# First chunk of a Mamba scan block: gate half of the input projection moved ahead, next chunk's norm moved ahead, first spreads on three queues

## The chip, the cores and the metric

The program runs on one core of one Trainium2 chip. The metric is the device time of the whole program in microseconds (us). The engines are TensorE (PE; its weight loads are shown as PEld), VectorE (DVE), ScalarE (ACT), GpSimd (POOL) and SyncE (SP), which only issues transfers here. A row's `granted clock` is the share of TensorE's full speed of 2.4 GHz: 1.00 is 2.4 GHz, 0.50 is 1.2 GHz.

## The reference

A decoder layer on x of 1 x 2048 x 256: x is added to a Mamba block, then to a cross attention over 1601 context rows, then to a mixture of experts. The change is in the Mamba block alone:

```python
x = x + _L0_attn_ref(_layernorm(x), W_in, conv_w, conv_b, W_x, W_dt, b_dt, A_log, D, W_out)

xz = x @ W_in                                   # 256 -> 1024
x_proj, z = jnp.split(xz, 2, axis=-1)           # 512 channels each
xc = causal depthwise convolution of x_proj, 4 taps
x_conv = silu(xc + conv_b)
dt_in, B_ssm = jnp.split(x_conv @ W_x, 2, -1)   # 16 each
dt = softplus(dt_in @ W_dt + b_dt)
A = -exp(A_log)                                 # 512 x 16
h = h * exp(dt * A) + dt * B * x_conv           # for each step, channel and state
y = sum over states of h + x_conv * D
return (y * silu(z)) @ W_out
```

## The kernel before

`scan_block` computes the Mamba block and takes the first half of the program; `attend_and_route` does the rest after it. The 2048 rows are taken in four chunks of 512 (`NQ = 4`, `CH = 512`, index q). The 512 channels are four blocks of 128 (`KM = 4`, index m). A chunk has 64 scans (`TILES = 64`), each of 128 (channel, state) pairs by 512 steps, numbered t = 0 to 255 over the four chunks. A tile t holds 32 channels by 4 states: n = t // 16 counts blocks of 128 channels, s = t // 4 groups of four scans that share four states, j = t % 4 the 32 channels.

For each scan t:
- ACT makes exp(dt * A) in a PSUM bank (L464), five banks ahead at most (`NDA = 5`: it waits for scan t - 5).
- POOL makes dt * B * x for two scans in one instruction (L296), from `rep` and `b_rep`.
- DVE scans (L567).
- After each four scans PE sums the states into a bank `psY` (`add_states`, L769 and L772). After sixteen of them DVE multiplies `psY` by silu(z) (`gate`, L524), at t = 18, 34, 50, 66 and so on, two scans after the sixteen end.

`rep` holds dt and u = dt * x_conv of each channel copied to four rows of partitions. It is filled by transfers from `dt_u` to `rep` (`spread`, L206): four of 128 KB for each j, sixteen for each n. All are issued by SP, except those of n = 0, j = 3, which POOL issues.

The work that prepares chunk q (`front`) lies among the scans of chunk q - 1 in an order written out by hand. Every step has a slot number k, and `front_time(q, k)` turns it into the scan t before or after which it stands on its engine: for q >= 2 it is 64 (q - 1) - 20 + k, for q = 1 it is 4 + k * 3 // 5. The steps are: transposes of the normed rows (`PE_XNT`), their copy to SBUF (`ACT_XT`, L350), the x half of the projection (`PE_X`, L608, copied by L320), the convolution as four matmuls with diagonal weights for each m (`PE_C`, L623, copied by L361), one silu over the four blocks with a table load before and after it (`ACT_SILU`, L366 and L367), the z half (`PE_Z`, L608, copied by L326), its silu with two table loads (`ACT_ZS`, L336 and L337), the small product (`PE_XS`), the spread of B (`PE_BR`, L332) and the softplus of dt (`PE_V`, `ACT_V`, `DVE_DT`). All of it uses two PSUM banks, `psF`. Each engine runs its own instructions in order, so a step that has to wait holds up all that stands behind it on its engine, the exps of ACT among them.

For the first chunk nothing can be hidden. In order: SP loads x (rows 0 to 511), the x half of `W_in`, the small tensors, the z half of `W_in`, the other 1536 rows, `W_out`. DVE takes the moments (L495, L498), POOL the power (L259, L261), DVE norms (L505) and copies `pick` out of `ident` (L532), while POOL builds `conv_d` (L271). PE transposes and makes the x half. ACT evacuates and makes the first tap (L438), DVE the other three (L538), twelve instructions. ACT's silu (L442) is followed by the small product (L643), its copy (L444), the step sizes (L653), the softplus on DVE and ACT (L552, L554, L448, L450, L516, L518) and the spread. After those PE makes the z half of chunk 0 (L608 again), ACT copies it between the first exps (`evac_z`, at t = 2, 3, 5, 6) and makes its silu at t = 12:

```python
ACT_Z0, ACT_ZS0 = (2, 3, 5, 6), 12
```

DVE takes the moments of chunk 1 after the convolution and norms its rows just before scan 0, where POOL has already made the power.

## Time and profile before

| | us |
|---|---|
| median of 3 runs | 770.64 (767.15 to 771.59) |
| the profiled execution, its time | 765.8 |
| its span in the trace | 764.0 |
| first scan starts | 49.25 |
| last scan ends | 409.3 |
| `attend_and_route` starts | 413.9 |

All rows are of one profiled execution. Its time is 1.8 us more than its span, and it is 4.8 us under the median of the three runs. A line of the timeline gives start, length, engine, line of code, operation and shapes, the count of instructions that are merged, and in brackets how long the engine was idle before it and what ended that.

### The profile page before, as it was taken

The numbers are of one execution on the slowest core, as the hardware profiler recorded it, in microseconds if no ns is written. First come the engines' busy times: TensorE is split into PE (matmuls) and PEld (weight loads), VectorE is DVE, ScalarE is ACT, GpSimd is POOL, SyncE is SP. The second block draws the span as 40 slices with busy tenths as digits, with TensorE's granted clock in tenths as the row PEclk, the third lists the DMA queues.
The fourth block names the chain that finished last, engine by engine and source line by source line (L and its number), as shares of the span: only waits on it lengthen the run. The fifth ranks groups of instructions, "written<-read, shape, count | busy, mean of one in ns | idle before, by whom it ended". The sixth has DMA issues, their size and how long they took to land. (4 is left out here: it accounts for less than half of the span.)

```text
span 764.0 us, 10447 instructions
## 1 busy us (share of the span) xinstructions
PE 636.9 (83%) x3130; PEld 399.2 (52%) x3130; DVE 591.7 (77%) x1040; ACT 445.8 (58%) x795; POOL 475.6 (62%) x391
## 2 busy tenths in 40 slices
PE   4589875997689975577889799999999989899990
PEld 2133212352133510043536799999998964688860
DVE  5787798889998999999887776767888777444327
ACT  2668799676987888848772445444445331444420
POOL 4069599978997999999873433232445347166550
PEclk9799985999869996579999999999999999999996
DMA  7092244325344352943322845442524033445318
GB/s 202 9 220 57 54 111 110 79 46 131 76 110 111 82 133 62 241 107 88 88 87 92 230 148 183 130 163 80 187 87 152 14 98 127 131 152 165 105 35 299
DMA packets 61604, 91.33 MB, mean 120 GB/s; under 512 B 13573, under 2 KB 46536, under 8 KB 61550
## 3 DMA queue, kind: packets, MB, share of 16 engines
q1 hardware_dynamic: 51278, 74.62, 37.5%
q0 software_dynamic: 3936, 8.72, 3.2%
q10 hardware_dynamic: 6336, 7.34, 2.7%
q8 instruction: 26, 0.43, 0.2%
q14 instruction: 28, 0.23, 0.1%
HBM read 36.54 MB, written 22.62 MB: 77 GB/s over the span
## 5 line engine op out<-in xcount | busy, mean ns | idle before, releaser
L296 POOL TENSOR_TENSOR b_in<-rep,b_rep 128x1024 f32<-128x1024 f32 x128 | 299.0, 2357 | 41.4 <-DVE h L567 34.4
L567 DVE TENSOR_TENSOR_SCAN h<-ps,hlast,b_in 128x512 f32<-128x512 f32 x256 | 306.4, 1264 | 16.9 <-ACT ps L464 10.0
L464 ACT ACTIVATE ps<-rep,neg_a 128x512 f32<-128x512 f32 x256 | 171.0, 684 | 42.7 <-DVE h L567 38.8
L772 PE MATMUL ps<-h,pick 128*32 128x512 f32 x512 | 80.5, 705 | 43.4 <-DVE h L567 43.1
L608 PE MATMUL ps<-xnT,w_in 128*128 128x512 f32 x128 | 68.4, 681 | 10.1 <-ACT xnT L350 4.1
L1071 POOL DMA_INDIRECT rows_by_token<-yt,yrow x46 | 44.7, 972 | 43.7 <-ACT yt L1183 19.0
L1212 DVE TENSOR_TENSOR p_lo<-ps,p_hi 128x512 fp32r<-128x512 f32 x64 | 35.1, 592 | 36.0 <-ACT p_hi L1082 36.0
L1480 PE MATMUL ps<-v_hi,p_hi 128*128 128x256 f32 x208 | 60.0, 288 | 1.2 <-DVE x_res L1335 1.2
L772 PEld LDWEIGHTS ps<-h,pick 128*32 128x32 f32 x512 | 10.7, 115 | 94.7 <-DVE h L567 85.0
L1480 PE MATMUL ps<-v_lo,p_hi 128*128 128x256 f32 x208 | 58.5, 281 | 0.0
L1480 PE MATMUL ps<-v_hi,p_lo 128*128 128x256 f32 x208 | 58.3, 280 | 0.0
L608 PEld LDWEIGHTS ps<-xnT,w_in 128*128 128x128 f32 x128 | 26.4, 217 | 51.7 <-issue 40.0
L1082 ACT ACTIVATE p_hi<-ps 128x512 fp32r<-128x512 f32 x64 | 30.0, 516 | 37.4 <-PE ps L1497 37.2
L1678 PE MATMUL ps<-w_exp,xT 128*128 x184 | 44.1, 383 | 0.0
L623 PE MATMUL ps<-xp,conv_d 128*128 128x512 f32 x96 | 43.8, 601 | 0.0
L1480 PE MATMUL ps<-c_hi,q_hi 128*128 128x512 f32 x96 | 41.0, 427 | 0.8 <-PEq L122 0.8
L1443 DVE TENSOR_TENSOR ht<-sgt,ps 128x256 f32<-128x256 f32 x23 | 9.7, 422 | 40.6 <-ACT sgt L1175 40.6
L1052 POOL TENSOR_TENSOR attn_rstd<-attn_mv,eps 128x1 f32<-128x1 f32 x14 | 4.1, 291 | 58.3 <-DVE attn_mv L1205 58.3
L1480 PEld LDWEIGHTS ps<-v_hi,p_hi 128*128 128x128 f32 x208 | 39.2, 188 | 1.4 <-DVE x_res L1335 1.4
L1044 POOL TENSOR_TENSOR rstd3s<-mv3s,eps 128x1 f32<-128x1 f32 x16 | 3.6, 223 | 57.5 <-DVE mv3s L1341 57.5
L1028 POOL DMA_INDIRECT rows_by_block<-xn,pos x32 | 32.4, 1013 | 11.1 <-issue 10.5
L1480 PEld LDWEIGHTS ps<-v_lo,p_hi 128*128 128x128 f32 x208 | 39.3, 189 | 0.0
(265 smaller groups left out, 1356.9 us busy)
## 6 DMA issues: line engine op xcount, KB each, us to landing
rep<-dt_u SPq DMA_DIRECT2D x252, 128.0 KB, 2.4
mask_sb<-in_mask_BxSxS_ik_dram SPq DMA_DIRECT2D x16, 800.5 KB, 4.6
xt<-rows_by_block SPq DMA_DIRECT2D x23, 258.0 KB, 2.8
rows_by_block<-pad SPq DMA_DIRECT2D x4, 1032.0 KB, 9.2
rows_by_token<-pad ACTq DMA_DIRECT2D x4, 1024.0 KB, 6.1
yb<-rows_by_token SPq DMA_DIRECT2D x4, 512.0 KB, 4.8
yb<-rows_by_token ACTq DMA_DIRECT2D x4, 512.0 KB, 5.6
w_exp<-L_ffn_expert_gate_w_dram SPq DMA_DIRECT2D x15, 128.0 KB
```

The source lines that it names most:

```text
L296: pool.tensor_tensor(b_in[:, (t - 1) % NB:(t - 1) % NB + 2, :], u_rep[:, n % 2, j - 1:j + 1, :], b_rep[q % 2][:, g, :].unsqueeze(1).to_bro ...
L464: act.activation(psA[:, t % NDA, :], dt_rep[:, n % 2, j, :], ACT.Exp, scale=neg_a[:, k:k + 1]).then_inc(exp_ready, 1)
L567: dve.tensor_tensor_scan(h[:, QC * (s % NH) + j, :], psA[:, t % NDA, :], b_in[:, t % NB, :], hlast[:, k:k + 1], ALU.mult, ALU.add).then_in ...
L608: last = pe.matmul(psF[:, m % 2, :], w_in[:, n, part * DI + m * P:part * DI + (m + 1) * P], xnT[:, n, :], start=(n == 0), stop=(n == KE - 1))
L623: last = pe.matmul(psF[:, m % 2, :], conv_d[:, m, n, :], xp[:, m, n:n + CH], start=(n == 0), stop=(n == NTAP - 1))
L772: last = pe.matmul(psY[32 * j:32 * j + 32, :], pick[:, :], h[:, QC * (s % NH) + j, :], start=False, stop=(g == NG - 1))
L1028: pool.indirect_dma_start(xs_dram[:, :], bass.IndirectOffsetOnAxis(ap=pos[:, t, k:k + 1], axis=0), xn3[:, t, :], None, bounds_check=NTILE ...
L1071: pool.indirect_dma_start(y_dram[:, :], bass.IndirectOffsetOnAxis(ap=yrow[:, 2 * s + a:2 * s + a + 1], axis=0), yt[:, s % YT, a, :], None, ...
L1082: act.activation(p_hi[:, a:b, :], psP[g % 2][:, 0:(b - a) * P], ACT.Copy).then_inc(pthi_ready, 1)
L1212: dve.tensor_tensor(p_lo[:, a:b, :], psP[g % 2][:, 0:(b - a) * P], p_hi[:, a:b, :].bitcast(F32), ALU.subtract).then_inc(ptlo_ready, 1)
L1480: mm = pe.matmul(out, stat[a], mov[b], start=first and n == 0, stop=last and n == 2)
L1678: last = pe.matmul(psG[i % 2][:, a * 2 * FI:(a + 1) * 2 * FI], xT[:, i % 2, cols], w_all[:, ds(e, 1), wcols].rearrange("p a n -> p (a n)") ...
```

## The change

1. The z half of chunk 0 is made right after the x half, straight into four of the five PSUM banks of the exps (the fourth block after the small product). ACT makes its silu from PSUM, block by block, among the silus of the convolution. The copies at t = 2, 3, 5, 6 and the silu with two table loads at t = 12 go.
2. The four step sizes of chunk 0 go to four different banks, one after another, and the four spreads of B follow.
3. DVE takes the moments of chunk 1, `neg_a` and the norm of chunk 1 before the convolution of chunk 0. POOL makes the power of chunk 1 before `conv_d`. The rows of chunk 1 are loaded by a transfer of their own, third in SP's order.
4. The first spreads: of j = 0 two transfers are issued by SP and two by ACT; j = 1 is issued by POOL, j = 2 and 3 by SP. POOL makes the first two scans' input one at a time.
5. Every step of `front(1)` stands three scans earlier: 1 + k * 3 // 5.

```diff
-ACT_Z0, ACT_ZS0 = (2, 3, 5, 6), 12
+POOL_J = 1
 def front_time(q, k):
-    return 4 + k * 3 // 5 if q == 1 else TILES * (q - 1) - SHIFT + k
+    return 1 + k * 3 // 5 if q == 1 else TILES * (q - 1) - SHIFT + k
+        psV = [psF[:, 1, :], psF[:, 0, :], psY, psA[:, KM, :]]
         # spread and SP
-        def spread(eng, n, j):
-            for r in range(QC):
+        def spread(eng, n, j, rows=range(QC)):
+            for r in rows:
             sp_.dma_start(w_in[:, :, 0:DI], ...).then_inc(s_win[0], 16)
+            sp_.dma_start(x_res[:, CHT:2 * CHT, :], xv[:, CHT:2 * CHT, :]).then_inc(x_next, 16)
...
-                for j in range(QC if n else QC - 1):
-                    spread(sp_, n, j)
+                for j in range(QC):
+                    if n == 0 and j == 0:
+                        spread(sp_, n, j, range(0, 2))
+                    elif n or j != POOL_J:
+                        spread(sp_, n, j)
         # gpsimd
             inverse_deviation(0)
-            pool.wait_ge(xn_ready, 1)
+            inverse_deviation(1)
             pool.wait_ge(s_conv, 16 * 2)
...
-            inverse_deviation(1)
             pool.wait_ge(u_ready, 1)
-            spread(pool, 0, QC - 1)
+            spread(pool, 0, POOL_J)
...
-                if j % 2:
+                if t < 2:
+                    pool.tensor_tensor(b_in[:, t, :], u_rep[:, 0, t, :], b_rep[0][:, 0, :], ALU.mult).then_inc(b_ready, 1)
+                elif j % 2:
         # scalar
-            for m in range(KM):
+            def silu_x0(m):
                 act.wait_ge(conv_done, m + 1)
                 act.activation(xc[0][:, m, :], xc[0][:, m, :], ACT.Silu).then_inc(xc_ready, 1)
+            def silu_z0(m):
+                act.wait_ge(z_ps, m + 1)
+                act.activation(zs[0][:, m, :], psA[:, m, :], ACT.Silu).then_inc(z_evac, 1)
+            silu_x0(0)
+            silu_x0(1)
+            silu_z0(0)
+            silu_x0(2)
+            silu_z0(1)
+            silu_x0(3)
+            silu_z0(2)
             act.wait_ge(xs_ps, 1)
             act.activation(xs[:, :], psF[:, 0, :], ACT.Copy).then_inc(xs_ready, 1)
+            silu_z0(3)
             act.preload_act_table_set("natural_log_exp_and_others")
...
+                if m == 1:
+                    act.wait_ge(u_ready, 1)
+                    spread(act, 0, 0, range(2, QC))
...
-                if t in ACT_Z0:
-                    evac_z(0, ACT_Z0.index(t))
-                if t == ACT_ZS0:
-                    silu_z(0)
         # vector: moments(1), neg_a and normalize(1) move from behind the convolution to ahead of it
-                dve.tensor_scalar(dt[:, m, :], psF[:, (m + 1) % 2, :], b_dt[:, m:m + 1], None, ALU.add).then_inc(v_evac, 1)
+                dve.tensor_scalar(dt[:, m, :], psV[m], b_dt[:, m:m + 1], None, ALU.add).then_inc(v_evac, 1)
         # tensor
+                    if q == 1:
+                        pe.wait_ge(br_ready, NG)
                     normal(q)
...
+            pe.wait_ge(s_win[1], 16)
+            for m in range(KM - 1):
+                w_in_product(psA[:, m, :], m, 1).then_inc(z_ps, 1)
             pe.wait_ge(s_small, 16 * 7)
             pe.wait_ge(x_evac, KM)
             small_product(0)
+            w_in_product(psA[:, KM - 1, :], KM - 1, 1).then_inc(z_ps, 1)
+            for m in range(KM):
+                step_size(0, m)
             pe.wait_ge(pick_ready, 2)
-            for m in range(KM):
-                ...
-                step_size(0, m)
-                if m % 2:
-                    pe.wait_ge(v_evac, m)
-                    spread_b(0, m - 1)
-                    pe.wait_ge(v_evac, m + 1)
-                    spread_b(0, m)
-            pe.wait_ge(s_win[1], 16)
-            for m in range(KM):
-                ...
-                w_in_product(m, 1).then_inc(z_ps, 1)
+            for g in range(NG):
+                if g < 2:
+                    pe.wait_ge(v_evac, g + 1)
+                else:
+                    pe.wait_ge(br_ready, g - 1)
+                spread_b(0, g)
+            pe.wait_ge(v_evac, KM)
```

## Rows read from the trace of the kernel before

**Rows 1.** What DVE waited for between the first and last scan, by releaser
```profile
DVE zs L524 <- PE ps L772: 13.9, 6, 4.8
```
**Rows 2.** Timeline of the first chunk's preparation, all engines
```profile
8.88 5.00 DVE L532 COPY pick<-ident 32x32 f32<-32x32 f32 x4
9.04 3.61 POOL L271 TENSOR_TENSOR conv_d<-ident,conv_w 128x2048 f32<-128x2048 f32 x1 [1.50 <-DVE xn L505]
...
12.25 10.16 PE L608 MATMUL ps<-xnT,w_in 128*128 128x512 f32 x16 [1.20 <-ACT xnT L430]
...
25.21 1.67 ACT L442 ACTIVATE xc<-xc 128x512 f32<-128x512 f32 x3
27.33 0.63 ACT L442 ACTIVATE xc<-xc 128x512 f32<-128x512 f32 x1 [0.45 <-DVE xc L538]
28.11 1.94 PE L643 MATMUL ps<-xc,w_x 128*32 128x512 f32 x8 [5.69 <-ACT xc L442]
...
30.84 3.75 PE L653 MATMUL ps<-xs,w_dt 128*128 128x512 f32 x4 [0.80 <-ACT xs L444]
...
32.92 0.75 DVE L552 TENSOR_SCALAR dt_u<-ps,b_dt 128x512 f32<-128x512 f32 x1 [3.12 <-PE ps L653]
...
36.74 0.69 DVE L518 TENSOR_TENSOR dt_u<-dt_u,xc 128x512 f32<-128x512 f32 x1
```
**Rows 3.** Same timeline from 44 us: spreads land, first scan
```profile
46.88 4.66 POOL L296 TENSOR_TENSOR b_in<-rep,b_rep 128x1024 f32<-128x1024 f32 x2 [6.87 <-DMA rep<-dt_u]
...
48.98 0.69 ACT L464 ACTIVATE ps<-rep,neg_a 128x512 f32<-128x512 f32 x1 [1.55 <-DMA rep<-dt_u]
```
**Rows 4.** DVE alone: the scans and their gaps
```profile
49.25 15.39 DVE L567 TENSOR_TENSOR_SCAN h<-ps,hlast,b_in 128x512 f32<-128x512 f32 x13 [3.18 <-POOL b_in L296]
68.30 4.82 DVE L567 TENSOR_TENSOR_SCAN h<-ps,hlast,b_in 128x512 f32<-128x512 f32 x4 [3.66 <-ACT ps L464]
...
78.82 0.69 DVE L524 TENSOR_TENSOR zs<-ps,zs 128x512 f32<-128x512 f32 x1 [1.90 <-PE ps L772]
...
89.05 3.63 DVE L567 TENSOR_TENSOR_SCAN h<-ps,hlast,b_in 128x512 f32<-128x512 f32 x3 [3.65 <-ACT hlast L468]
...
155.16 0.69 DVE L524 TENSOR_TENSOR zs<-ps,zs 128x512 f32<-128x512 f32 x1 [4.81 <-PE ps L772]
```
**Rows 5.** PE alone, chunk 0's scans
```profile
54.73 1.06 PE L772 MATMUL ps<-h,pick 128*32 128x512 f32 x8
...
57.93 3.70 PE L608 MATMUL ps<-xnT,w_in 128*128 128x512 f32 x8 [1.11 <-ACT xnT L350]
...
74.16 3.60 PE L623 MATMUL ps<-xp,conv_d 128*128 128x512 f32 x8
77.69 1.06 PE L772 MATMUL ps<-h,pick 128*32 128x512 f32 x8
...
96.50 1.04 PE L643 MATMUL ps<-xc,w_x 128*32 128x512 f32 x8
```
**Rows 6.** Windows: length, busy time by engine, granted clock, DMA share, GB/s
```profile
25.00:26.00 1.00, 0.00 (x0) 0.00 (x0) 0.96 (x3) 0.99 (x3) 0.00 (x0) 0.62 0.00 0
...
28.10:34.70 6.60, 5.79 (x13) 1.98 (x14) 3.14 (x13) 2.15 (x3) 1.29 (x2) 0.50 0.00 1
```
**Rows 7.** Transfers between 43 and 52 us, all queues
```profile
DMA packets 774, 2.09 MB, mean 233 GB/s; under 512 B 263, under 2 KB 263, under 8 KB 774
```
**Rows 8.** Loads up to 50 us: KB each, median us to landing
```profile
w_in<-in_L_attn_W_in_dram SPq DMA_DIRECT2D x2, 512.0 KB, 4.6
```
**Rows 9.** ACT alone: exps, last conv copy, first exp after silu, chunk 2's rows
```profile
68.70 1.90 ACT L464 ACTIVATE ps<-rep,neg_a 128x512 f32<-128x512 f32 x3
...
82.42 0.69 ACT L361 ACTIVATE xc<-ps,conv_b 128x512 f32<-128x512 f32 x1 [2.75 <-PE ps L623]
...
88.23 0.69 ACT L464 ACTIVATE ps<-rep,neg_a 128x512 f32<-128x512 f32 x1
...
128.98 1.00 ACT L350 ACTIVATE xnT<-ps 128x1024 f32<-128x1024 f32 x1
```

More of the change, by code:

```diff
@@ L198, in rep_sem @@
         def rep_sem(n, j):
-            return rep_pool if n == 0 and j == QC - 1 else rep_in[n % 2][j]
+            return rep_pool if n == 0 and j == POOL_J else rep_in[n % 2][j]
         def rep_count(n, j):
-            return (n // 2 + (0 if j == QC - 1 and n % 2 == 0 and n else 1)) * QC * 16
-        def spread(eng, n, j):
-            for r in range(QC):
+            return (n // 2 + (0 if j == POOL_J and n % 2 == 0 and n else 1)) * QC * 16
+        def spread(eng, n, j, rows=range(QC)):
+            for r in rows:
                 eng.dma_start(rep[32 * r:32 * r + 32, n % 2, j, :, :],
@@ L227, in _ @@
             sp_.dma_start(w_in[:, :, DI:], w["W_in"][:, DI:].rearrange("(k p) n -> p k n", p=P)).then_inc(s_win[1], 16)
[L228 to L229 removed]
+            sp_.dma_start(x_res[:, 2 * CHT:, :], xv[:, 2 * CHT:, :]).then_inc(s_rest, 16)
+            sp_.dma_start(w_out[:, :, :], w["W_out"].rearrange("(m p) n -> p m n", p=P)).then_inc(s_rest, 16)
             for n in range(KM * NQ):
@@ L453, in _ @@
                     evac_b(0, m)
+            act.wait_ge(z_evac, KM)
             act.wait_ge(ident_ok, 2)
@@ L491, in moments @@
             def moments(q):
-                dve.wait_ge(x_in if q == 0 else x_rest, 16)
+                dve.wait_ge(*((x_in, 16), (x_next, 16), (s_rest, 32))[min(q, 2)])
                 dve.wait_ge(xn_ready, q)
@@ L522, in gate @@
                 dve.wait_ge(summed, NG * (n + 1))
-                dve.wait_ge(zs_ready, q + 1)
+                if q:
+                    dve.wait_ge(zs_ready, q)
+                else:
+                    dve.wait_ge(z_evac, KM)
                 dve.tensor_tensor(zs[q % 2][:, m, :], psY, zs[q % 2][:, m, :], ALU.mult).then_inc(gated, 1)
@@ L533, in _ @@
             last.then_inc(pick_ready, 1)
+            moments(1)
+            dve.wait_ge(a_exp, 1)
+            for r in range(QC):
+                rows = slice(32 * r, 32 * r + 32)
+                dst = neg_a[rows, :].rearrange("p (b g j) -> p b g j", b=KM, g=NG)
+                src = a_log[rows, :, :].rearrange("p (b j) (g n) -> p n b g j", b=KM, n=QC)[:, r]
+                last = dve.tensor_scalar(dst, src, -1.0, None, ALU.mult)
+            last.then_inc(consts_ready, 1)
+            normalize(1)
             for m in range(KM):
@@ L541, in _ @@
                 last.then_inc(conv_done, 1)
-            moments(1)
-            dve.wait_ge(a_exp, 1)
-            for r in range(QC):
-                rows = slice(32 * r, 32 * r + 32)
-                dst = neg_a[rows, :].rearrange("p (b g j) -> p b g j", b=KM, g=NG)
-                src = a_log[rows, :, :].rearrange("p (b j) (g n) -> p n b g j", b=KM, n=QC)[:, r]
-                last = dve.tensor_scalar(dst, src, -1.0, None, ALU.mult)
-            last.then_inc(consts_ready, 1)
             for m in range(KM):
                 dve.wait_ge(v_ps, m + 1)
-                dve.tensor_scalar(dt[:, m, :], psF[:, (m + 1) % 2, :], b_dt[:, m:m + 1], None, ALU.add).then_inc(v_evac, 1)
+                dve.tensor_scalar(dt[:, m, :], psV[m], b_dt[:, m:m + 1], None, ALU.add).then_inc(v_evac, 1)
                 dve.wait_ge(v_evac, m + 1)
@@ L557, in _ @@
                     step_and_input(m)
-            normalize(1)
             for t in range(TILES * NQ):
@@ L604, in normal, with w_in_product @@
                 last.then_inc(xnT_ps, 1)
-            def w_in_product(m, part):
+            def w_in_product(out, m, part):
                 for n in range(KE):
-                    last = pe.matmul(psF[:, m % 2, :], w_in[:, n, part * DI + m * P:part * DI + (m + 1) * P], xnT[:, n, :],
+                    last = pe.matmul(out, w_in[:, n, part * DI + m * P:part * DI + (m + 1) * P], xnT[:, n, :],
                                      start=(n == 0), stop=(n == KE - 1))
@@ L617, in x_part @@
                     pe.wait_ge(x_evac, m - 1)
-                w_in_product(m, 0).then_inc(x_ps, 1)
+                w_in_product(psF[:, m % 2, :], m, 0).then_inc(x_ps, 1)
             def convolve(q, m):
@@ L627, in project @@
                 pe.wait_ge(gated, KM * (q + 1))
-                pe.wait_ge(s_wout, 16)
+                pe.wait_ge(s_rest, 32)
                 for m in range(KM):
@@ L652, in step_size @@
                     pe.wait_ge(br_ready, NG * q + m + 3)
-                pe.matmul(psF[:, (m + 1) % 2, :], w_dt[:, m * P:(m + 1) * P], xs[:, :], start=True, stop=True).then_inc(v_ps, 1)
+                pe.matmul(psF[:, (m + 1) % 2, :] if q else psV[m], w_dt[:, m * P:(m + 1) * P], xs[:, :], start=True, stop=True).then_inc(v_ps, 1)
             def spread_b(q, g):
@@ L692, in front @@
                         pe.wait_ge(c_evac, 3 + m)
-                    w_in_product(m, 1).then_inc(z_ps, 1)
+                    w_in_product(psF[:, m % 2, :], m, 1).then_inc(z_ps, 1)
                 if k == PE_XS:
```

14 lines of the change are left out of this document (2 added, 12 removed).

## The prediction

> **What bounds the kernel now.** I first read the timeline for where the scan block starts its scans and ends: scan 0 starts at 49.25 us, scan 255 ends at 409.3. Before that the first chunk is a chain through all engines, with nothing else to do. In between DVE is nearly always scanning. Thirteen scans take 15.39 us, 1.18 us each [rows 4]; POOL, at 4.66 us for four scans' input, runs at the same 1.17 [rows 3]. So I asked next what DVE waits for. The largest sum is the gate, 13.9 us in six waits, for PE's sums of the states [rows 1]. The change can win in two places: the chain up to scan 0, and the gap of 3.66 us ahead of scan 13, where ACT is away for the silu of z with two table loads [rows 4]. Behind these stand three waits that decide what of it arrives. Gate 0 waits 1.90 us for PE at 78.82; scan 24 waits 3.65 us, because ACT is in the silu of the convolution; gate 3 waits 4.81 us for PE at 155.16 [rows 4]. A gain of DVE that ends in one of them is lost. What reaches the end of the block is what PE gains at gate 3, and nothing after that depends on absolute time.
>
> **The change, step 1: up to the first spread.** ACT is first in line. It makes three silus at 0.56 us each (1.67 / 3), is idle 0.45 us until the convolution ends, and makes the last one at 27.33 [rows 2]. Two silus of z now stand ahead of that one: 2 x 0.56 - 0.45 = 0.67 us later. The small product follows. PE had been idle 5.69 us before it [rows 2], its granted clock had fallen to 0.62 in the window at 25 us and stood at 0.50 until 34.7 [rows 6]. So its eight passes took 1.94 us, where eight at full clock take 1.04 [rows 5]. With three z blocks of 1.77 us each (half of a pair's 3.54, below) PE is busy until about 27.6 and idle only about 1.2 us. I take full clock: -0.90. The step sizes used to start 0.79 us after the product (30.84 - 30.05, the copy by ACT); now the fourth z block lies between, 1.77 us: +0.98. The first step size reaches DVE 2.08 us after its start at half clock [rows 2]; it has two passes, each of which loses about 0.43 us when the clock is full: -0.87. The second is then in its bank when DVE wants it; DVE waited 0.23 for it, -0.25. Sum: 0.67 - 0.90 + 0.98 - 0.87 - 0.25 = -0.4 us. The spread, issued at 37.46 when u of block 0 is ready (36.74 + 0.69) [rows 2], is issued at 37.1. Hidden: table load and z silu of block 3 lie under the step size and DVE's first two instructions. With the clock at half the three PE terms would be +0.90 (the product), +1.77 (the z block) and +0.87 (the step size): 3.5 us more.
>
> Moved ahead of the convolution: moments, `neg_a` and norm of chunk 1, 1.8 + 0.9 + 1.4 us on DVE between the picks and the first tap at 17.6. Room is there if nothing blocks. POOL's `conv_d` now runs from about 12.8 to 16.4 instead of 9.0 to 12.7. It took 3.61 us, and the four small copies of `pick` beside it took 5.00 us instead of under a microsecond [rows 2]. These are free now; `neg_a` and the norm lie beside `conv_d` instead. Whether they are held up like a copy no row shows: between 0 and, if the first tap waits for all of POOL's three instructions and then the norm, 1.3 us on the convolution's end, of which ACT's own 0.67 hides half: 0 to 0.65. I take 0, since the norm's 128 x 256 ran at 0.35 us apiece like an instruction at single rate. The Trainium skill (SBUF — State Buffer, on the port pair that DVE and GpSimd share) says that an exclusive lock holds off a DVE instruction in a two-port mode, or with two SBUF inputs, while GpSimd works. The copies agree with it (3.6 us held up); if it also held the norm and first tap the sum would be 0.65 us worse. The extra transfer third in SP's queue puts all behind it back by one issue, 0.5 us; the z half of `W_in`, issued at 9.8 and 4.6 us on its way [rows 8], lands near 15 and isn't wanted before the x half ends at 22.4 [rows 2]; `conv_w`, near 7, isn't wanted before 12.8.
>
> **Step 2: the spreads.** Sixteen transfers of 128 KB make 2.1 MB. From the first issue at 37.46 to the last exp that waited for them (48.98) [rows 3] are 11.5 us, with all queues together at 233 GB/s [rows 7]: 9.0 us plus 2 until the first byte. More queues change the order, not the rate. So j = 0 and 1 come earlier, scans 0 and 1 start at about 45 and 46, but j = 3 lands 11.0 to 11.5 us after the first issue, at 48.3, whoever issues it. POOL then needs 2.33 us for scans 2 and 3: scan 2 at 50.6 instead of 51.6. From there POOL feeds DVE at DVE's own pace, so only 1.0 us is left of 4. The rule of the Trainium skill (DMA: Bandwidth & Descriptors, Issuing engines are not separate DMA queues) is the same: it saves issue time alone. By it, too, the sum is that of the rows. ACT's two issues (about 1.3 us) hold up its copies of B; nobody waits for these before 43.
>
> **Step 3: PE through chunk 0, the step that decides.** Scan 3 ends at 53.0, and PE sums group 0 at once (1.0 us; 54.73 before [rows 5]), as the z blocks no longer stand ahead of it. Then the front of chunk 1. From the first x block at 57.93 to the sum of group 3 at 77.69 PE had no idle time shown: four x blocks, three convolution blocks and two sums in 19.76 us [rows 5]. With the front three scans earlier the fourth convolution block stands before the sum of group 3 (slot 14 instead of 17, the sum at 16), at 3.53 us (77.69 - 74.16). So 54.0 + 19.8 + 3.5 = 77.3 at full clock. The clock isn't full: PE's last work before is the transposes at about 44 to 46, then it waits some 7 us for scan 3. Before the z blocks filled that place. After an idle time of 5.69 us the clock stood at 0.50 for 6.6 us, 28.1 to 34.7, until it was busy again [rows 6]. Half of such a stretch is lost: 3.3 us at most, 0 if the clock doesn't fall. I take 2.5, as PE is now densely busy. The fourth convolution ends at 79.8 (82.2 before), the sum of group 3 at 80.8, and gate 0 is at 80.9 instead of 78.82. DVE has finished scan 18 about 9 us earlier or stands behind ACT, which waits in order for the convolution's blocks. The 3.66 us and the 1.0 us end here.
>
> **Step 4: ACT to the rows of chunk 2.** The copy of the last convolution block goes from 82.42 to 80.0; from it to the first exp after the silu are 5.8 us [rows 9], so 85.8 instead of 88.23. But that exp is number 21, not 24, three more at 0.63 (1.90 / 3 [rows 9]): exp 24 at 87.7, 0.5 us early. From here to 128.98 ACT was nearly never idle: it sets the pace. Its work there is the same, but three scans earlier the copies meet PE waiting for scans: I count 1.3 us for the fourth z block and 1.4 to 1.8 for B and the first dt, against some 2 us of such waits before. Estimate 1.0 more, 0 to 2. Chunk 2's rows are copied at 129.5 instead of 128.98 [rows 9].
>
> **Step 5.** PE works from there to gate 3 without a free stretch, and DVE has 4.81 us to spare [rows 4]. So gate 3, and the end, come **0.5 us later**. The profiled execution's own time is 765.8, so 766.3; on the median, 770.64 + 0.5 = 771.1.
>
> **The rivals.**
> - *Everything arrives.* PE's clock stays up and ACT and PE catch up by themselves, so DVE keeps 1.0 us of the start and the 3.66 us of the gap: -4.7, 765.9. For it: the z work really leaves ACT (four copies, a silu, two table loads). Against it: the order at gate 0, and the 4.81 at gate 3, where DVE has slack already.
> - *Part arrives.* The clock doesn't fall ahead of the first sum, or rises at once: 2.5 less, -2.0, 768.6.
> - *Slower: PE cold at the small product.* If 1.2 us of idle time and ACT's later silu are enough for the clock to be at 0.50 at 28.8, step 1 is 3.5 us longer, and all behind it moves with it: 0.5 + 3.5 = +4.0, 774.7. It decides from a granted clock below about 0.6 there. Against it: the clock was still full 2.9 us after PE's last matmul (idle from 22.4 [rows 2], 0.62 in the window from 25 on [rows 6]).
> - *The change doesn't fill the wait.* If the z half of `W_in` landed after 22.4 it would; it lands 7 us before. Under 0.02.
>
> **How the numbers follow.** My forecast, -1.2 to +2.0 (bounds of the clock, the port and ACT's waits), 0.50. Part arrives, down to -3.8: 0.17. Everything: 0.13. Slower by 2.0 to 3.8 for mixed bounds: 0.08; cold PE: 0.12. 0.5% of the time, 3.85 us, is about what a measurement can tell from no change: faster 0.13, same 0.75, slower 0.12. The range leaves out the case where everything arrives and goes to the cold case: 766.8 to 774.8.
>
> **What would show it.** Right: the spread issued near 37; scan 0 near 45, scan 2 near 50.6; a granted clock of 1.00 at the small product and 0.5 at 53; a wait of DVE before 80 of some 9 us in all, gate 0 at 81; the first exp after the silu at 85.8; chunk 2's rows at 129.5. Wrong: gate 0 before 78; ACT not back to back between 90 and 125; gate 3's wait gone, because then DVE's gains count as well.

## The result and the profile after

| | before | after |
|---|---|---|
| median of 18 runs, us | 769.82 (767.15 to 773.34) | 772.36 (769.45 to 774.67) |
| profiled execution, span, us | 764.0 | 769.9 |

The changed kernel takes 2.5 us more. The ratio is 1.0032 with a 95% interval of 1.0018 to 1.0046, so 1.4 to 3.5 us more: a small loss, under 0.5% of the time, but clear of noise. 0.5 us more had been forecast. All ratios here are of the fast executions alone, which leaves out one single execution, of the kernel best below, that took 3450 us.

The two profiled executions are 5.9 us apart, more than the medians, and 4.3 of that lie behind the scan block, where no line differs. The profiled execution of before (765.8 us, span 764.0) is quicker than all of its 18 runs in the table, so the profiles are compared here only inside the scan block. *Gate n* is DVE's n-th product of the summed states with silu(z), from 0 to 15; a chunk has four.

First DVE alone, the scans (L590) and the gate (L547). It answers to [rows 4].

```profile
44.89 1.27 DVE L590 TENSOR_TENSOR_SCAN h<-ps,hlast,b_in 128x512 f32<-128x512 f32 x1
46.37 1.28 DVE L590 TENSOR_TENSOR_SCAN h<-ps,hlast,b_in 128x512 f32<-128x512 f32 x1 [0.21 <-POOL b_in L298]
50.87 7.16 DVE L590 TENSOR_TENSOR_SCAN h<-ps,hlast,b_in 128x512 f32<-128x512 f32 x6 [3.21 <-POOL b_in L302]
...
71.83 1.28 DVE L590 TENSOR_TENSOR_SCAN h<-ps,hlast,b_in 128x512 f32<-128x512 f32 x1 [2.62 <-ACT ps L488]
...
81.36 0.69 DVE L547 TENSOR_TENSOR zs<-ps,zs 128x512 f32<-128x512 f32 x1 [1.81 <-PE ps L797]
81.97 2.45 DVE L590 TENSOR_TENSOR_SCAN h<-ps,hlast,b_in 128x512 f32<-128x512 f32 x2
87.06 7.16 DVE L590 TENSOR_TENSOR_SCAN h<-ps,hlast,b_in 128x512 f32<-128x512 f32 x6 [2.64 <-ACT ps L488]
...
155.50 0.69 DVE L547 TENSOR_TENSOR zs<-ps,zs 128x512 f32<-128x512 f32 x1 [3.54 <-PE ps L797]
```

Scan 0 starts 4.4 us earlier than before, scan 2 about 0.7, and the gap of 3.66 us ahead of scan 13 is gone. Six smaller waits for ACT stand between scan 2 and gate 0 instead, 8.0 us together, and gate 0 is 2.5 us later. At gate 3 the kernels are 0.3 us apart (155.50 against 155.16). The cause of the late gate stands in PE's rows [rows 5]:

```profile
44.58 1.02 PE L794 MATMUL ps<-xc,skip_d 128*128 128x512 f32 x2
53.38 1.93 PE L797 MATMUL ps<-h,pick 128*32 128x512 f32 x8 [7.78 <-DVE h L590]
55.24 5.50 PE L631 MATMUL ps<-xnT,w_in 128*128 128x512 f32 x8
...
73.16 7.14 PE L646 MATMUL ps<-xp,conv_d 128*128 128x512 f32 x16
80.23 1.06 PE L797 MATMUL ps<-h,pick 128*32 128x512 f32 x8
```

PE is idle for 7.78 us before the sum of group 0. The sum then takes 1.93 us instead of 1.06, and the first x blocks 5.50 instead of 3.70. The last two convolution blocks (7.14 us) stand together ahead of the sum of group 3. The granted clock in windows of 2 or 3 us (the last but two column; [rows 6]):

```profile
45.00:48.00 3.00, 0.60 (x2) 0.00 (x0) 2.44 (x2) 1.38 (x2) 1.26 (x1) 1.00 0.92 214
...
52.00:54.00 2.00, 0.62 (x4) 0.20 (x8) 2.00 (x3) 0.73 (x2) 2.00 (x2) 0.50 0.90 217
...
58.00:60.00 2.00, 2.00 (x5) 0.92 (x4) 0.03 (x1) 0.94 (x2) 2.00 (x1) 0.78 0.00 0
60.00:62.00 2.00, 2.00 (x6) 0.89 (x5) 1.28 (x1) 1.59 (x5) 2.00 (x2) 1.00 0.00 0
```

And the first chunk's preparation, all engines [rows 2]:

```profile
12.46 5.03 DVE L563 TENSOR_SCALAR neg_a<-a_log 32x64 f32<-32x64 f32 x4 [0.99 <-ACT a_log L438]
12.80 3.61 POOL L276 TENSOR_TENSOR conv_d<-ident,conv_w 128x2048 f32<-128x2048 f32 x1
...
19.00 9.03 DVE L570 SCALAR_TENSOR_TENSOR xc<-xp,conv_w,xc 128x512 f32<-128x512 f32 x12
...
28.06 0.63 ACT L449 ACTIVATE xc<-xc 128x512 f32<-128x512 f32 x1 [0.45 <-DVE xc L570]
...
28.84 1.06 PE L666 MATMUL ps<-xc,w_x 128*32 128x512 f32 x8 [1.51 <-ACT xc L449]
```

`neg_a` took 5.03 us beside `conv_d` and the `skip_d` that follows it on POOL (to 17.4) where it had needed under one, and the taps start at 19.00 instead of 17.6.

### The profile page after: what moved, and what is told of

Its sections match the earlier page's. It is cut to its first block and busy times, and to the rows that moved or that the text cites. A ratio compares the mean times of both kernels' runs of the same rounds, so it can differ in the third digit from the quotient of the medians.

```text
span 769.9 us, 10444 instructions
## 1 busy us (share of the span) xinstructions
PE 632.2 (82%) x3130; PEld 398.3 (52%) x3130; DVE 593.3 (77%) x1040; ACT 441.4 (57%) x792; POOL 475.5 (62%) x392
## 5 line engine op out<-in xcount | busy, mean ns | idle before, releaser
L590 DVE TENSOR_TENSOR_SCAN h<-ps,hlast,b_in 128x512 f32<-128x512 f32 x256 | 306.5, 1265 | 19.9 <-ACT ps L488 16.5
L631 PE MATMUL ps<-xnT,w_in 128*128 128x512 f32 x128 | 66.4, 667 | 2.8 <-ACT zs L332 1.5
L1500 PEld LDWEIGHTS ps<-v_hi,p_lo 128*128 128x128 f32 x208 | 39.2, 188 | 0.0
```

The costliest lines, as they stand in the source:

```text
L590: dve.tensor_tensor_scan(h[:, QC * (s % NH) + j, :], psA[:, t % NDA, :], b_in[:, t % NB, :], hlast[:, k:k + 1], ALU.mult, ALU.add).then_in ...
L631: last = pe.matmul(out, w_in[:, n, part * DI + m * P:part * DI + (m + 1) * P], xnT[:, n, :], start=(n == 0), stop=(n == KE - 1))
L1500: mm = pe.matmul(out, stat[a], mov[b], start=first and n == 0, stop=last and n == 2)
```

## The experiments

Twelve more runs were made, in three groups, each beside the kernel before on the same chip. All edits are to the changed kernel unless a line says otherwise. Times in the table are those of one profiled execution each; the ratio is to the kernel before, over several runs. "First spread" is the issue of its first transfer, "rows of chunk 2" ACT's copy of that chunk's transposed rows. warm, order, shift4 and unlock ran on one chip, port, early, nospread and after2 on a second, fill, early_port, best and before2 on a third. The changed kernel itself has a ratio only beside the second group (after2) and from the first measurement (after); a ratio of the first or third group set against it is a comparison of different chips.

| kernel | first spread | gate 0 | rows of chunk 2 | gate 3 | last gate | ratio (95%) |
|---|---|---|---|---|---|---|
| before | 37.46 | 78.82 | 128.98 | 155.16 | 410.60 | 1 |
| before2 (the same) | 36.49 | 79.52 | 129.68 | 155.65 | 410.93 | 1.0000 (0.9987 to 1.0014) |
| after | 36.99 | 81.36 | 130.13 | 155.50 | 412.23 | 1.0032 (1.0018 to 1.0046) |
| after2 (the same) | 36.93 | 80.94 | 129.72 | 154.84 | 411.42 | 1.0024 (1.0009 to 1.0040) |
| warm | 37.03 | 79.51 | 129.91 | 155.42 | 409.93 | 1.0021 (1.0007 to 1.0035) |
| order | 37.05 | 79.12 | 132.63 | 157.96 | 414.62 | 1.0075 (1.0049 to 1.0100) |
| shift4 | 36.87 | 79.31 | 131.07 | 157.04 | 412.31 | 1.0056 (1.0040 to 1.0073) |
| unlock | 38.88 | 83.44 | 132.22 | 157.51 | 414.18 | 1.0041 (1.0024 to 1.0057) |
| port | 35.76 | 80.19 | 128.97 | 154.30 | 411.01 | 0.9986 (0.9968 to 1.0005) |
| nospread | 38.42 | 82.44 | 131.22 | 157.96 | 413.74 | 1.0039 (1.0020 to 1.0057) |
| fill | 37.18 | 81.50 | 130.27 | 155.58 | 412.25 | 1.0039 (1.0025 to 1.0053) |
| early | 38.56 | 77.42 | 126.18 | 152.76 | 408.47 | 0.9931 (0.9906 to 0.9955) |
| early_port | 36.33 | 75.28 | 124.06 | 150.70 | 406.42 | 0.9952 (0.9936 to 0.9969) |
| best | 36.20 | 77.73 | 126.52 | 151.77 | 408.43 | 0.9980 (0.9965 to 0.9995) |

**warm: filling work in the wait for scan 3.**

```diff
+                    if s == 0:
+                        for _ in range(8):
+                            pe.matmul(psY, ident[:, :], w_in[:, 0, 0:CH], start=True, stop=True)
                     pe.matmul(psY, skip_d[:, n % KM, :], ...)
```

> The changed kernel with eight extra 128x512 products by PE into the bank psY ahead of the first skip product; their result is overwritten and nothing else changes. They fill the 7.8 us that PE waits for scan 3. Theory (PE's work from scan 3 to gate 0, then ACT's, sets the end; half clock from 53.4 to about 59 costs 2.7 us): granted clock 1.00 at 53.4, gate 0 at about 78.6 instead of 81.4, chunk 2's rows copied at about 127.5 instead of 130.1, gate 3 some 2.5 us earlier, median 2.5 us under the changed kernel. Rival (the early part is hidden behind the later waits, what was lost lies elsewhere): gate 3 and the median within 0.5 us of the changed kernel.

The idle time before the sum of group 0 fell to 1.69 us, the sum took 1.07 instead of 1.93, the x blocks 3.70 instead of 5.50. From the start of that sum to gate 0 are 25.3 us here and 28.0 in the changed kernel, so the low clock costs 2.7 us, as the theory has it (2.2 in after2, whose x blocks took 5.01). Gate 0 itself came only 1.85 us earlier, because the sum started 0.8 later: the spread landed later in this execution, as the exps that waited for it show. ACT alone, first of the changed kernel, then of the kernel warm:

```profile
48.36 1.91 ACT L488 ACTIVATE ps<-rep,neg_a 128x512 f32<-128x512 f32 x3 [1.49 <-DMA rep<-dt_u]
49.16 1.91 ACT L488 ACTIVATE ps<-rep,neg_a 128x512 f32<-128x512 f32 x3 [2.11 <-DMA rep<-dt_u]
```

The 1.85 us held until 96 us on all engines. Then 1.6 of them were lost in PE's spread of B, which took 5.42 us here and 3.80 in the changed kernel. PE alone, then windows of 2 us, of the kernel warm:

```profile
54.19 1.07 PE L800 MATMUL ps<-h,pick 128*32 128x512 f32 x8 [1.69 <-DVE h L590]
55.19 3.70 PE L631 MATMUL ps<-xnT,w_in 128*128 128x512 f32 x8
...
96.29 5.42 PE L681 MATMUL ps<-xs,pick_b 128*128 128x512 f32 x8
```
```profile
94.00:96.00 2.00, 0.70 (x8) 0.16 (x8) 2.00 (x4) 2.00 (x4) 0.59 (x1) 1.00 0.00 0
96.00:98.00 2.00, 2.00 (x7) 0.68 (x4) 2.00 (x3) 0.28 (x2) 1.92 (x2) 0.63 0.58 131
98.00:100.00 2.00, 2.00 (x4) 0.93 (x3) 2.00 (x3) 0.66 (x2) 1.82 (x4) 0.52 0.88 199
```

So the cost of the clock at 53 us is shown (2.7 us; 2.5 had been forecast). That it reaches the end isn't shown: at gate 3 warm is 0.1 us earlier, the clock having fallen at another place instead, and the ratio is 0.2 to 0.8 us better than those of after2 and after, within all the intervals and on another chip.

**order: the fourth convolution block behind the sum of group 3.**

```diff
-    return 1 + k * 3 // 5 if q == 1 else TILES * (q - 1) - SHIFT + k
+    return 1 + k * 3 // 5 + 2 * (k == 23) if q == 1 else TILES * (q - 1) - SHIFT + k
```

> The changed kernel with the fourth convolution block of chunk 1 (and ACT's fourth copy of x) two scans later, behind the sum of group 3, as it stood in the kernel before. Theory A (ACT's chain from the last convolution block sets the end): gate 0 3.5 us earlier, at 77.9, but the last block 1.0 us later, so silu, chunk 2's rows and gate 3 1.0 us later, median up to 1 us more than the changed kernel. Rival B (gate 0's wait for PE is the loss): gate 3 and the median some 3 us less.

Gate 0 came 2.2 us earlier and had nothing to wait for, and gate 3 came 2.5 us later. By the ratios the kernel is 3 to 4 us slower than the changed one, where theory A had up to 1; the interval, 1.0049 to 1.0100, lies above both of those of the changed kernel, though from another chip. DVE alone, of the kernel order:

```profile
79.12 0.67 DVE L547 TENSOR_TENSOR zs<-ps,zs 128x512 f32<-128x512 f32 x1
79.70 1.27 DVE L590 TENSOR_TENSOR_SCAN h<-ps,hlast,b_in 128x512 f32<-128x512 f32 x1
82.58 1.28 DVE L590 TENSOR_TENSOR_SCAN h<-ps,hlast,b_in 128x512 f32<-128x512 f32 x1 [1.60 <-ACT hlast L492]
87.90 7.16 DVE L590 TENSOR_TENSOR_SCAN h<-ps,hlast,b_in 128x512 f32<-128x512 f32 x6 [4.04 <-ACT ps L488]
```

The wait has moved to ACT, which stands behind the last convolution block: the first exp after the silu is at 87.11 instead of 86.27. Rival B falls. Of the 2.5 us at gate 3 this is 0.84; nearly all the rest came at the spread of B (5.38 us instead of 3.80), as in warm.

**shift4: the front of chunk 1 where it was.**

```diff
-    return 1 + k * 3 // 5 if q == 1 else TILES * (q - 1) - SHIFT + k
+    return 4 + k * 3 // 5 if q == 1 else TILES * (q - 1) - SHIFT + k
```

> The changed kernel with front(1) back where it was (4 + k*3//5); z half, norm and spreads stay as changed. PE idles on after the sum of group 0 until chunk 1's rows are transposed (t = 4) and copied (t = 8). Theory: x half starts near 58 as before, the clock is at half there too, gate 0 near 80 to 81, last convolution block 3 us later than in the changed kernel, gate 3 later by 0 to 3 us; median 0 to 3 us above the changed kernel. Rival (the earlier slots crowd PE and ACT and are themselves the loss): median 2 us or more below the changed kernel.

1.5 us later at gate 3, as the theory has it, and 1.0056 against 1.0032 and 1.0024 by the ratios, which is 1.8 to 2.5 us slower, from another chip and with intervals that meet. So the rival, that the earlier slots are themselves the loss, falls. That they gain something up to gate 3 is shown; what they are worth to the end isn't. At the last gate shift4 has 412.31 and the changed kernel 412.23 and 411.42, since shift4 is spared a fall of the clock at 358 us that the changed kernel has (below).

**unlock and port: POOL's work away from DVE's.** unlock adds one wait ahead of `conv_d`; port moves `pick_b` up behind the picks and `conv_d` and `skip_d` behind the convolution.

```diff
             inverse_deviation(1)
+            pool.wait_ge(xn_ready, 2)             # unlock
---
             inverse_deviation(0)
+            pool.wait_ge(pick_ready, 1)           # port
+            pool.tensor_copy(pick_b[:, :, :], ...).then_inc(pick_ready, 1)
             inverse_deviation(1)
+            pool.wait_ge(conv_done, KM)
             pool.wait_ge(s_conv, 16 * 2)
```

> The changed kernel with one wait more: POOL starts conv_d only when DVE has normed chunk 1. Theory (DVE's neg_a and norm were held up by conv_d: 5.03 and 1.56 us instead of about 0.9 and 1.4): neg_a under 1 us, norm ends near 15, first tap at 17.6, convolution ends at 27.3 instead of 28.0, spread issued about 0.5 us earlier and everything with it, median 0.5 us less. Rival (the lock is not what held neg_a): neg_a as long as before, no change.

`neg_a` took 0.87 us, so it had been held by POOL's work: the theory's first half. The second half failed. Now the taps lie beside POOL's three instructions, and both sides are held. All engines, of the kernel unlock:

```profile
12.53 0.87 DVE L564 TENSOR_SCALAR neg_a<-a_log 32x64 f32<-32x64 f32 x4 [0.99 <-ACT a_log L439]
...
17.66 10.55 DVE L571 SCALAR_TENSOR_TENSOR xc<-xp,conv_w,xc 128x512 f32<-128x512 f32 x12 [2.85 <-ACT xc L445]
...
18.45 1.49 POOL L282 TENSOR_TENSOR skip_d<-ident,d_skip 128x512 f32<-128x512 f32 x1
...
29.02 1.07 PE L667 MATMUL ps<-xc,w_x 128*32 128x512 f32 x8 [2.39 <-ACT xc L450]
30.02 3.68 PE L632 MATMUL ps<-xnT,w_in 128*128 128x512 f32 x4
```

Twelve taps took 10.55 us instead of 9.03, `skip_d` 1.49 instead of 1.04. The convolution ends at 28.2, no earlier than with `neg_a` held (28.0). The spread was issued 1.9 us later, for another reason: the fourth z block took 3.68 us instead of 1.98, at a granted clock of 0.55 in the window from 30 to 31.

> The changed kernel with POOL's work moved away from DVE's: pick_b right after the picks, conv_d and skip_d after the convolution has ended. Theory (DVE's neg_a and norm are held by conv_d, and its taps, which read two tensors in SBUF, by skip_d and pick_b): neg_a 0.9 us, norm ends near 15, first tap 17.6, convolution ends at 27.3 without a held tap, PE idle about 1 us before the small product at full clock, spread issued at 36.3 to 36.6 instead of 37.0, gate 3 0.5 us earlier, median 0.5 us under the changed kernel. Rival (only the first wait counts, as with the norm ahead of conv_d): spread after 38 again.

Here nothing is held. All engines, of the kernel port:

```profile
17.47 9.04 DVE L571 SCALAR_TENSOR_TENSOR xc<-xp,conv_w,xc 128x512 f32<-128x512 f32 x12 [2.84 <-ACT xc L445]
...
26.59 3.61 POOL L279 TENSOR_TENSOR conv_d<-ident,conv_w 128x2048 f32<-128x2048 f32 x1 [13.86 <-DVE xc L571]
...
27.60 1.06 PE L667 MATMUL ps<-xc,w_x 128*32 128x512 f32 x8 [0.95 <-ACT xc L450]
```

The convolution ends at 26.5, 1.5 us earlier than in the changed kernel. The spread is issued 1.2 us earlier, and gates 0 and 3 come 1.2 us earlier (0.75 and 0.5 against after2). Twice what had been expected, since the taps of port follow one another without a wait, which those of before did not. Part of this belongs to the execution: ACT's second copy of x stood at 18.11 here and at 18.78 in the changed kernel. In early_port and best, which move POOL's work too and have that copy at 18.68 and 18.55, the convolution ends at 27.0 and 26.8 and the spread is issued 0.7 and 0.8 us earlier than in the changed kernel. The hold costs 0.7 to 1.2 us at the spread. The ratio on the same chip went from 1.0024 to 0.9986, 2.9 us with intervals that just don't meet, where 0.5 had been expected. The profile shows no more than 1.2 of it; where the rest comes from isn't shown. PE's short idle time before the small product, 0.95 us, may spare port the late spreads that are told of under fill.

**nospread: the first spreads as before.**

```diff
-POOL_J = 1
+POOL_J = 3
-                if m == 1:
-                    act.wait_ge(u_ready, 1)
-                    spread(act, 0, 0, range(2, QC))
-                if t < 2: ... one scan at a time
```

> The changed kernel with the first spreads as before: j = 0, 1, 2 by SP, j = 3 by POOL, none by ACT, and POOL's input two scans at a time from the start. Theory (2.1 MB at the rate of the 16 DMA engines are the limit, not the issue): scan 0 near 48.8 instead of 44.9, but scan 2 at 51.0 to 51.3 instead of 50.9, gate 0, gate 3 and the median within 0.5 us of the changed kernel. Rival (the three queues bring the spreads in earlier): scan 2 more than 1 us later and the median 1 us or more higher.

This execution issued its spread late (38.42), so distances are read from there. All engines, of the kernel nospread:

```profile
38.42 15.13 SPq L207 DMA_DIRECT2D rep<-dt_u  x23
...
47.85 6.94 POOL L298 TENSOR_TENSOR b_in<-rep,b_rep 128x1024 f32<-128x1024 f32 x3 [6.88 <-DMA rep<-dt_u]
...
50.22 3.63 DVE L583 TENSOR_TENSOR_SCAN h<-ps,hlast,b_in 128x512 f32<-128x512 f32 x3 [4.88 <-POOL b_in L298]
```

Scan 0 starts 11.8 us after the first issue, against 7.9 in the changed kernel. Scan 2, two scans of 1.18 us later, starts at 52.6, so 14.2 after it; in the changed kernel it is 13.9 (50.87 - 36.99). Three queues instead of two bring scan 0 forward by 3.9 us and scan 2 by 0.3: up to gate 0 the theory holds. Gate 3 lies 2.5 us behind the changed kernel's, where 0.5 had been allowed: 1.1 stand at gate 0 and at the rows of chunk 2 already, with the late spread, and 1.4 came with the first x blocks of chunk 2, which took 6.45 us instead of 5.07. The ratio, 1.0039, lies 1.2 us above that of after2 with intervals that overlap; since this profile has two other losses in it, the runs can't give that to the spreads.

**fill: no idle time before the small product.** In unlock, early and nospread the clock fell between 28 and 31 us and the spread came 1.4 to 1.9 us late. PE's idle time before the small product was 2.39, 2.19 and 2.90 us there. It was 0.95 to 2.08 in after, after2, warm, order, shift4 and port, where the clock stayed at 1.00.

```diff
+            for _ in range(2):
+                pe.matmul(psA[:, KM - 1, :], ident[:, :], w_in[:, 0, 0:CH], start=True, stop=True)
             pe.wait_ge(s_small, 16 * 7)
```

> The changed kernel with two 128x512 products by PE ahead of the small product, into the bank that the fourth z block overwrites. PE's idle time there was 1.5 to 2.1 us in the profiles with the clock at 1.00 until the step sizes, and 2.2 to 2.9 us in the three (unlock, early, nospread) in which it fell before or under the fourth z block and the spread was issued 1.5 to 1.9 us later. Theory (this is a part of the loss, in about one execution of three): idle time under 1.2 us, granted clock 1.00 from 26 to 31 us, spread at 37.0 or earlier, median 0.4 to 1.0 us under the changed kernel. Rival (the late spread is swallowed later): no change of the median.

Inconclusive. The small product and the z block ran at full clock, but the filling work ended at 29.0, later than the silu, and held the small product back 0.2 us. One profile can't show that something stopped which happens in one execution of three, and the ratio, 1.0039 (five runs, another chip), is no better than the changed kernel's. Nor does the idle time alone decide it. Before its second pair of B's spreads PE was idle for 2.22 to 2.24 us in eleven profiles; in ten of them the four passes took 1.98 or 1.99 us, at full clock, and in early_port 3.56 us, at a granted clock of 0.58 from 38 to 40.

**early: real work in the wait for scan 3.** ACT copies chunk 1's transposed rows at t = 1, and PE makes the first two x blocks at t = 2.

```diff
+FIRST = {5: 2, 6: 2, 7: 1, 11: 4}
 def front_time(q, k):
+    if q == 1 and k in FIRST:
+        return FIRST[k]
```

> The changed kernel with real work in PE's 7.8 us ahead of the sum of group 0: chunk 1's transposed rows are copied by ACT at t = 1 and its first two x blocks are made at t = 2. Theory (PE's work and half clock between scan 3 and the last convolution block set the end): these blocks run at 47 to 51, last convolution block 5 to 6 us earlier, gate 0 near 75.5 instead of 81.4, silu of the convolution from 76 on. ACT and DVE then set the pace: chunk 2's rows at 124.5 to 128 instead of 130.1, gate 3 3 to 5 us earlier, median 2 to 5 us under the changed kernel. Rival (later waits swallow it, as they did 1.7 of the 1.9 us that the filling products gained at gate 0): chunk 2's rows within 0.5 us, median within 1 us of the changed kernel.

PE alone, of the kernel early:

```profile
48.19 6.55 PE L634 MATMUL ps<-xnT,w_in 128*128 128x512 f32 x8 [1.89 <-ACT xnT L359]
...
55.53 1.06 PE L800 MATMUL ps<-h,pick 128*32 128x512 f32 x8
56.53 3.70 PE L649 MATMUL ps<-xp,conv_d 128*128 128x512 f32 x8
...
76.28 1.07 PE L800 MATMUL ps<-h,pick 128*32 128x512 f32 x8
```

The blocks still run at half clock (6.55 us), but where nobody waits, and the sum of group 0 and the convolution have the full clock. Although the spread was 1.6 us late in this execution, gate 0, chunk 2's rows and gate 3 came 3.9, 3.9 and 2.7 us earlier. On the same chip the ratio fell from 1.0024 to 0.9931, 7.2 us; it beats the kernel before by 5.3 us. That is more than the 2 to 5 us expected. Of the 5.2 us between the profiled executions of after2 and early, 2.9 stand at the last gate, though the spread was 1.6 late, and 2.3 behind the scan block, where no line differs. early is also spared the fall of the clock at 358 us (below), worth 1.7.

**early_port and best.** early_port joins the two. best adds one filling product ahead of the small product and three ahead of the skip product.

> The kernels early and port together: chunk 1's first x blocks ahead of the sum of group 0, and POOL's work away from DVE's. Theory (the two gains are of different stretches and add up): spread near 35.8, gate 0 near 74.7, chunk 2's rows near 123.5, gate 3 near 150, median 7 to 10 us under the changed kernel, 5 to 7.5 us under the kernel before (ratio 0.990 to 0.9935). Rival (the later waits swallow the second gain): no better than early, ratio 0.993 to 0.995.

In the profile the gains add up, and the spread is not late in this execution: against the changed kernel gate 0 is 6.1 us earlier, gate 3 4.8 us, the last gate 5.8. By the ratios the sum isn't there: 0.9952, 3.7 us under the kernel before where 5 to 7.5 had been expected, while early alone had 0.9931 on another chip. The intervals overlap between 0.9936 and 0.9955. Both are faster than either kernel; which of the two is the faster is open.

> early_port with one filling product ahead of the small product and three ahead of the skip product of group 0, so that PE's clock doesn't fall in either wait. Theory (the clock costs what is left at both places): granted clock 1.00 from 26 us to the first convolution block, sum of group 0 at full clock, ratio to the kernel before 0.5 to 1.5 us better than early_port's. Rival (nothing is late there any more): the same as early_port within 0.3 us.

Worse by 2.1 us, and the profile shows why. PE alone, of the kernel best; L800 is the filling work:

```profile
46.00 6.48 PE L635 MATMUL ps<-xnT,w_in 128*128 128x512 f32 x8 [2.05 <-ACT xnT L360]
52.32 2.74 PE L800 MATMUL ps<-w_in,ident 128*128 128x512 f32 x6
54.89 1.02 PE L801 MATMUL ps<-xc,skip_d 128*128 128x512 f32 x2
55.85 1.06 PE L804 MATMUL ps<-h,pick 128*32 128x512 f32 x8
```

At half clock the x blocks already reach up to 52.3, just before scan 3 ends. The filling work now stands in the path, and the sum of group 0 is at 55.85 instead of 53.40. Of these 2.45 us gate 3 keeps 1.1; at the last gate it is 2.0 again, as best has the fall of the clock at 358 us and early_port hasn't (below). Theory and rival both fall.

**after2 and before2: what one profile is worth.**

> The changed kernel itself once more, for the scatter of a profile. The first profiled execution had 1.6 us more than the kernel before up to the end of the scan block and 4.3 us more behind it, where no line differs. Theory (the 4.3 us are scatter of one execution, as PE's clock falls and rises at other places): behind the scan block 350 to 352 us, as in the kernels warm, unlock, order and shift4; scan block's last gate at 412 to 413. Rival (the changed kernel's second half is really longer): 353 us or more again.

> The kernel before once more, for the scatter of a profile on the same chip as the others. The part behind the scan block was 350.2 us in its first profile and 350 to 351 in warm, unlock, order and shift4, but 352 to 356 in after, after2, port, early and nospread, which ran beside a slower median of the kernel before. Theory (this part belongs to the chip and the execution, not to the change): whatever it is here, it agrees within 1.5 us with that of fill, early_port and best, which run on this chip. Last gate of the scan block at 410 to 411, the one before last with a wait of 2.4 or of 4.1 us. Rival: 350 here and 353 or more in the changed ones.

The first profile of the changed kernel was 4.3 us longer than that of before behind the scan block, where no line differs. after2 had it again (354.7 us from the last residual to the end of the span, 354.5 in after, 350.2 in before): its theory, 350 to 352, was wrong as it stood. But the kernels of the same group had 354.5 (port), 352.4 (early) and 356.0 (nospread), those of the first group 350.2 to 351.2, those of the third 350.6 (before2), 351.4, 350.4 and 351.1. before2 held to its theory: 350.6 beside 350.4 to 351.4. So this part goes with the group and not with the change. The kernel before itself tells the same: its median is 770.2 in the second group and 765.8 and 765.6 in the others. That it is the chip is likely, but group and chip changed together, and the first profile of before, 350.2, has no changed kernel with that value beside it. Ratios compare on one chip only.

Two profiles of one kernel also differ inside the scan block: before and before2 by 1.0, 0.7, 0.7 and 0.5 us at the first spread, gate 0, chunk 2's rows and gate 3, after and after2 by 0.1, 0.4, 0.4 and 0.7. Differences of that size between single profiles show nothing.

## Why the prediction was right, and where it was too small

**Up to gate 3 the order of events held.** The spread was forecast at 37.1 and was at 36.99; scan 2 at 50.6 and 50.87; gate 0 at 80.9 and 81.36; the first exp after the silu at 85.8 and 86.27; chunk 2's rows at 129.5 and 130.13; gate 3 0.5 us later than before and 0.34 later. The step that decided it, the fourth convolution block and a cold PE between scan 3 and gate 0, is shown by warm (the clock costs 2.7 us, 2.5 had been forecast) and by order (moving the block off gate 0 loses at gate 3 instead of gaining, 0.8 us by ACT's later silu and the rest by a fall of the clock). That the gains of DVE end there is shown by early: its scan 2 starts 1.7 us later than the changed kernel's (52.54), and gate 0, behind PE's earlier work, comes 3.9 us earlier. The program is 7.2 us faster than the changed kernel on the same chip.

**The total was less well forecast than the range says.** +2.5 us lies within 766.8 to 774.8, but outside the -1.2 to +2.0 of the main forecast; it falls in "slower by 2.0 to 3.8 for mixed bounds", which had 0.08. The 0.34 at gate 3 is partly luck. The rows of chunk 2 were 1.15 us late, not 0.5. Behind them the first x blocks took 5.07 us instead of 5.89, at a granted clock of 1.00 instead of 0.88 from 134 to 136, which the prediction hadn't counted. And after2 and before2 have gate 3 the other way round, 154.84 against 155.65: no difference is shown there.

**Step 1 was right in its sum, by two terms that were wrong.** That is luck. The wait for POOL was taken at 0, at most 0.65. It cost 1.5 us of the convolution against port (26.5 and 28.0), 1.1 and 1.2 against early_port and best, and 0.7 to 1.2 at the spread. The Trainium skill (SBUF — State Buffer, Who interferes with whom) had named it, as the prediction says: a DVE instruction in a two-port mode, or with two inputs in SBUF, and a GpSimd one that reads SBUF block each other. The runs agree: `neg_a`, a tensor_scalar, took 5.03 us beside `conv_d` and `skip_d` and 0.87 ahead of them, and the taps, with two tensors in SBUF, took 10.55 beside POOL's work (unlock) and 9.04 away from it (port). That `neg_a` ran in a two-port mode no row shows. My reading of the norm's 0.35 us as a sign against it was no evidence. Against that stood a start of the convolution that could have been earlier than I took it: without the hold it ends at 26.5 to 27.0, not at 27.3, because the copies of x came sooner. That part of the chain differs by as much in the kernel before itself: sixteen passes of its x half took 10.16 us in one profile and 8.61 in the other, and the first spread was issued at 37.46 and at 36.49.

**The cold-PE rival had a chance of 0.12 as a state of the kernel; it is an event of single executions.** The clock fell before or under the fourth z block in three of the nine profiles of the changed kernel and its variants, up to the second group, and cost 1.4 to 1.9 us each time. The rival put it at 3.5, with all three products at half clock; in unlock and early the small product still ran at the full one. As an average 1.7 / 3 = 0.6 us might be due to it. That is an estimate: fill, made to test it, showed nothing.

**Step 5 was wrong.** It said that nothing changes behind gate 3 ("nothing after that depends on absolute time"). From gate 3 to the last gate the kernel before takes 255.4 us, before2 255.3, and shift4, early and early_port 255.3 to 255.7. after takes 256.7, and after2, order, unlock, port, fill and best 256.6 to 256.7. nospread and warm, with 255.8 and 254.5, stand apart. So the changed kernel loses another 1.3 us, in both of its profiles. It is made of two parts. 1.7 us are lost in one place, PE's products of the weights at 358 us, ahead of the last gate but two: from the gate before it to this one are 23.6 us in the nine kernels after, after2, warm, order, unlock, port, nospread, fill and best, and 21.9 in before, before2, shift4, early and early_port. And 0.4 us are won between gates 6 and 7 (22.96 us instead of 23.38), where the granted clock from 222 to 224 is 0.82 instead of 0.70. PE's products and DVE's wait at that gate, the kernel after:

```profile
358.23 2.81 PE L750 MATMUL ps<-w_qkv_raw 128*128 128x256 f32 x8 [1.01 <-ACT c_all L424]
360.84 1.91 PE L755 MATMUL ps<-w_qkv_raw,bk 128*128 128x256 f32 x4
...
371.44 0.69 DVE L547 TENSOR_TENSOR zs<-ps,zs 128x512 f32<-128x512 f32 x1 [4.09 <-PE ps L797]
```
And the kernel before, the same:
```profile
358.29 2.00 PE L725 MATMUL ps<-w_qkv_raw 128*128 128x256 f32 x8 [1.01 <-ACT c_all L418]
360.12 1.03 PE L730 MATMUL ps<-w_qkv_raw,bk 128*128 128x256 f32 x4
...
369.82 0.69 DVE L524 TENSOR_TENSOR zs<-ps,zs 128x512 f32<-128x512 f32 x1 [2.41 <-PE ps L772]
```

The granted clock from 360 to 365 is 0.73 after and 1.00 before, with PE's work the same in both and 0.06 us apart. Why it falls in the one and not in the other stays open. It isn't the z half, the norm or the spreads by themselves, for shift4 has them all and no fall. Behind gate 3, then, the clock decides: -0.4 and +1.7 us. Together: nothing that is shown at gate 3, 1.3 behind it, and perhaps 0.6 from the executions with a cold PE make 1.9 us of the measured 2.5 (1.4 to 3.5). The first pair of profiles has 1.6 us at the last gate, after2 and before2, from two chips, 0.5. The rest has no place.

**The other rivals.** *Everything arrives* and *part arrives* fell: gate 0 was late, and even warm, which kept the clock up to gate 0, had it 0.7 us later than before, level with before2, and stayed above the kernel before by its ratio. What warm would be if its clock had not fallen at 96 us no run shows. *The change doesn't fill the wait* fell: the z blocks end at 27.3.

## What to carry to other kernels

Work that looks misplaced, as the z blocks did between the first scans, may be what keeps PE's clock up there. Before work is moved out of an engine's wait, ask what that engine will have left to do in it, and put its next real work in that place (early), not filling work, which stands in the way as soon as its guess of the idle time is wrong (best). When a front is moved forward by one number, each of its steps passes other work; look at what now stands ahead of each sum or gate. And a step that is moved along DVE lands beside other work of POOL, which can hold it up: `neg_a` cost nothing where it stood. Last, an effect of 1 or 2 us is read neither from one profile nor from ratios of different chips.

## What the runs showed of the hardware that was not expected

- DVE and POOL hold each other up in more pairs than I had counted: four tensor_scalar of 32 x 64 took 5.03 us beside two POOL tensor_tensor (`conv_d` and `skip_d`) instead of 0.87; twelve scalar_tensor_tensor of 128 x 512 took 10.55 us instead of 9.03, and POOL's product beside them 1.49 instead of 1.04.
- The same program on the same input has the clock fall at different places from one execution to the next: the two passes of the skip product at 44.6 us took 1.02 us in after and 1.92 in after2. And it falls at the same place in one kernel after another: at the products of the weights near 358 us in nine profiles of fourteen. A lead of 1.85 us shrank to 0.1 by a fall that the changed kernel doesn't have (warm, at 96 us).
- Part of a program that no line of the change touches took 350.2 to 351.4 us in two groups of runs and 352.4 to 356.0 in the other.
